# Attention scores in 32-row strips of the array, transposes in one PSUM bank, four rotating banks, and a new written-out order

## The reference

```python
h = tok(x)                                    # (32, 38, 256): layernorm, W, layernorm, + positions
h = h + attn0(layernorm(h))                   # causal; quantised w_attn, w_proj
h = h + tanh(layernorm(h) @ weight @ aux1 @ aux2 + bias)
h = h + attn1(layernorm(h))                   # not causal; biases, head mask
h = h + moe(layernorm(h))                     # softmax gate, top 1 of 16, capacity 76, two matrices

def attn(x):                                  # per image and head
    att = softmax(q @ k.T / 4 (+ causal mask))     # 38 x 38
    return concat_heads(att @ v) @ w_out
```

## Time and profile before

| | |
|---|---|
| times of three runs without a profile | 348.88, 349.08, 351.28 us; median 349.08 |
| span of the profiled execution, first to last instruction | 353.6 us |
| busy: TensorE, VectorE, ScalarE, GpSimd | 94%, 57%, 48%, 47% |
| instructions | 8931, of them 3254 matmul records and as many weight loads |

### The profile page before, as it was taken

One profiled execution on the slowest core, in us unless ns is written; L12 is line 12 of the kernel. 1 busy time (PEld: TensorE's weight loads), 2 busy tenths in 40 slices (PEclk: granted clock), 3 DMA queues, 4 the chain that ended last, 5 costly groups with the idle time before them and its releaser, 6 DMA issues.

```text
span 353.6 us, 8931 instructions
## 1 busy us (share of the span) xinstructions
PE 331.0 (94%) x3254; PEld 240.4 (68%) x3254; DVE 201.4 (57%) x525; ACT 169.6 (48%) x483; POOL 165.1 (47%) x280
## 2 busy tenths in 40 slices
PE   4979999999889999999999988979999999999993
PEld 3867887878768688888888866768455455464361
DVE  4469588455638856586676799770243351361350
ACT  0568824856246575676665555540243342441340
POOL 2166559946467787498776664661002102012012
PEclk9996999999989999999999999868999999999998
DMA  7999007213464157185312214115999998992400
GB/s 225 412 395 406 21 28 256 72 53 108 135 197 164 58 184 246 57 271 168 112 55 87 83 56 163 50 51 167 390 379 408 344 374 346 340 356 101 149 11 12
DMA packets 40155, 66.24 MB, mean 187 GB/s; under 512 B 4831, under 2 KB 30920, under 8 KB 39760
## 3 DMA queue, kind: packets, MB, share of 16 engines
q1 hardware_dynamic: 35832, 56.37, 46.0%
q10 hardware_dynamic: 2632, 7.05, 5.3%
q0 software_dynamic: 1648, 2.24, 1.9%
HBM read 54.17 MB, written 8.48 MB: 177 GB/s over the span
## 4 chain that ended last, share of the span: by engine, by line
PE 73%; SPq 10%; issue 6%; DVE 5%; POOL 2%; DMA 2%; ACT 1%; DVEq 0%; POOLq 0%; ACTq 0%
PE bank L1101 12%; PE bank L1068 12%; SPq L744 10%; PE bank L932 8%; PE bank L956 6%; PE bank L1023 4%; PE bank L967 4%; PE bank L1079 3%; PE bank L1007 3%; PE bank L986 3%; PE bank L996 3%; PE bank L1030 3%; PE bank L1107 2%; PE bank L941 2%; PE bank L890 2%
## 5 line engine op out<-in xcount | busy, mean ns | idle before, releaser
L857 POOL DMA_INDIRECT out<-mid,idx x12 | 11.7, 976 | 97.9 <-DVE mid L1479 97.0
L1101 PE MATMUL bank<-early,mid 128*64 128x256 f32 (+1 forms) x448 | 43.7, 381 | 0.0
L827 POOL TENSOR_TENSOR mid<-mid,tab 128x608 f32<-128x608 f32 x32 | 38.7, 1211 | 4.5 <-PE bank L986 2.2
L1261 ACT ACTIVATE mid<-bank,cols 128x64 f32<-128x64 f32 (+1 forms) x128 | 25.8, 332 | 25.1 <-PE bank L1079 25.1
L1068 PE MATMUL bank<-early,mid 128*64 128x512 f32 (+1 forms) x192 | 36.2, 596 | 0.7 <-ACT mid L1244 0.7
L1101 PEld LDWEIGHTS bank<-early,mid 128*64 128x64 f32 (+1 forms) x448 | 25.3, 123 | 15.8 <-issue 2.9
L1383 DVE TENSOR_REDUCE mx<-bank 102x16 f32<-102x608 f32 x32 | 25.2, 787 | 17.6 <-PE bank L986 17.3
L956 PE MATMUL bank<-xnT,attn 128*128 128x256 f32 (+1 forms) x160 | 35.1, 372 | 0.0
L956 PEld LDWEIGHTS bank<-xnT,attn 128*128 128x128 f32 x160 | 29.0, 190 | 3.9 <-issue 0.6
L812 POOL TENSOR_TENSOR rs<-rs,mhalf 128x1 f32<-128x1 f32 (+2 forms) x50 | 28.8, 576 | 4.2
L932 PE MATMUL bank<-early 128*128 128x256 f32 (+2 forms) x120 | 29.9, 410 | 0.0
(11 more groups left out here) (153 smaller groups left out, 669.1 us busy)
## 6 DMA issues: line engine op xcount, KB each, us to landing
early<-in_w SPq DMA_DIRECT2D x52, 512.0 KB, 7.1
v3a<-vt SPq DMA_DIRECT2D x102, 40.0 KB
early<-vt SPq DMA_DIRECT2D x90, 40.0 KB
expert_in<-k_empty SPq DMA_DIRECT2D x6, 514.0 KB, 4.9
early<-in_xf SPq DMA_DIRECT2D x4, 768.0 KB, 17.0
early<-in_xt ACTq DMA_DIRECT2D x4, 768.0 KB, 23.0
xnT<-in_w SPq DMA_DIRECT2D x4, 512.0 KB
tokens<-in_w SPq DMA_DIRECT2D x4, 512.0 KB
```

What stands on the lines that cost most here:

```text
L827: eng.tensor_tensor(km[:, n % 2], bc(kT[:, :, n * PCOLS:(n + 1) * PCOLS], 2, 4), bc(bc(quarterm[:, :], 2, PCOLS), 1, KC), ALU.mult).then_i ...
L1101: ins = mm(Yp[m % 2][a * width:(a + 1) * width, 0:DIM], hT[:, m % 2, c, a * width:(a + 1) * width], w2s[e % W2_SLOTS][:, c, :], start=c == ...
L1261: ins = eng.activation(hT[:, m % 2, c, a * width:(a + 1) * width], Tp[0][:, c * 128 + a * width:c * 128 + (a + 1) * width], ACT.Relu, bias ...
```

## The change

Scores go in 32-row strips. `score_order` puts two heads into each 32-row strip of features, `km` holds two copies instead of four, and the scores of a pair are 16 matmuls of 2 x 38 = 76 columns (eight before, of 152), which go to four PSUM banks, one per strip, and two halves of the partitions: eight tiles of the array where there were four. The causal mask of layer 0 comes in two parts of 32 query rows: 16 bf16 matmuls of 152 columns (four before, of 304).

PSUM: four banks `low` for the scores, four banks `high` for a rotation of four. The transposes of the probabilities are packed, 76 columns apart, into one bank, with a permuted identity `pack` that puts the pair's 76 real columns first; `pt` and `pv` have no banks of their own any more and take turns in the rotation. VectorE takes the reciprocal in two halves. The planner knows a cost of switching TensorE between full array, score strips and value product, and all wishes have new numbers, so all lists are new.

```diff
-GOAL = {"exp": 89.3, "z": 175.2, "xs": -251.3, "tabs": -0.2, "cs": -328.8, "bs": 60.1, "asum": 171.8, "qs": -234.6, "fB": -330.4,
+GOAL = {"exp": 118.7, "z": 240.6, "xs": -207.7, "tabs": 174.3, "cs": 34.3, "bs": -74.3, "asum": -274.8, "qs": -1652.0, "fB": 155.3,
...
+MODE, SWITCH = {"s": 1, "pv": 2}, 0.09
...
-           "ffn": "dve", "log": "act", "cnt": "dve", "v": "act", "qk": "act"}
+           "ffn": "dve", "log": "act", "cnt": "dve", "v": "act", "qk": "act", "pt": "act", "pv": "dve"}
...
-    f, r, i, d = np.meshgrid(np.arange(KC), np.arange(2), np.arange(4), np.arange(HD), indexing="ij")
-    return w[..., ((8 * r + 4 * f + i) * HD + d).reshape(-1)]
+    f, g, i, d = np.meshgrid(np.arange(KC), np.arange(4), np.arange(2), np.arange(HD), indexing="ij")
+    return w[..., ((4 * g + 2 * f + i) * HD + d).reshape(-1)]
...
-        return max([at] + [end[d] + (0.06 if d[0] == e else HANDOVER[d[0]]) for d in before])
+        at = max([at] + [end[d] + (0.06 if d[0] == e else HANDOVER[d[0]]) for d in before])
+        return at + SWITCH if e == "pe" and MODE.get(kind, 0) != mode[0] else at
...
-        Sp = bank[0][:, :].rearrange("p (f n) -> p f n", f=2)
-        PTp = bank[1][:, :].rearrange("p (j n) -> p j n", j=8)
-        Op = bank[2][:, 512:1024]
...
-        G = [bank[3][:, 0:512], bank[3][:, 512:1024], bank[2][:, 0:512]]
...
+        Sp = low[:, :].rearrange("p (g n) -> p g n", g=4)
...
+        G = [high[:, 512 * b:512 * (b + 1)] for b in range(SLOTS_G)]
...
                     if l == 0:
-                        for r, r0, r1, q, key in corners:
-                            mm(Sp[r0:r1, r, 0:8 * SEQ], identb[BROW * r:BROW * (r + 1), BROW * r:BROW * r + r1 - r0], causb[BROW * r:BROW * (r + 1), :],
-                               start=True, stop=False, skip_group_check=True)
+                        for part in range(2):
+                            for g, strip, r0, r1, q, key in corners:
+                                mm(Sp[r0:r1, g, 0:4 * SEQ], selb[strip, part, 0:r1 - r0], causb[strip, part, :],
+                                   start=part == 0, stop=False, skip_group_check=True)
                     for f in range(KC):
-                        for r, r0, r1, q, key in corners:
-                            half = slice(BROW * r, BROW * (r + 1))
-                            ins = mm(Sp[r0:r1, r, 4 * f * SEQ:4 * (f + 1) * SEQ], qT[half, f, q], km[half, n % 2, f, :, key],
+                        for g, strip, r0, r1, q, key in corners:
+                            ins = mm(Sp[r0:r1, g, 2 * f * SEQ:2 * (f + 1) * SEQ], qT[strip, f, q], km[strip, n % 2, f, :, key],
                                      start=l == 1, stop=True, skip_group_check=True)
...
-                    if m > 1:
-                        pe.wait_ge(pt_ready, m - 1)
-                    else:
-                        pe.wait_ge(tables_used, 2)
+                    ps, full = take(uses[(kind, l, n)])
                     for j in range(6):
-                        ins = tr(PTp[0:KROWS, j, 0:PROWS], P[0:PROWS, n % 2, HSTART[j]:HSTART[j] + 3, :], ident[0:PROWS, 0:PROWS])
+
+                        ins = tr(ps[0:KROWS, j * PCOLS:j * PCOLS + PROWS], P[0:PROWS, n % 2, HSTART[j]:HSTART[j] + 3, :], pack[0:PROWS, :])
...
-                    link(eng.reciprocal(rec[:, n % 2, :], ov[:, :, HD]))
+                    ov = G[b][0:PROWS, 0:HEADS * VW].rearrange("p (h d) -> p h d", h=HEADS)
+                    eng.reciprocal(rec[0:SEQ, n % 2, :], ov[0:SEQ, :, HD])
+                    link(eng.reciprocal(rec[BROW:PROWS, n % 2, :], ov[BROW:PROWS, :, HD]))
```

More of the change, by code:

```diff
@@ L48 @@
 BROW = 64
+QROW = 32
 PROWS = BROW + SEQ
@@ L68 @@
 SLOTS = 4
+SLOTS_G = 4
 EPS = 1e-5
@@ L83, in constants @@
     head[p, p // HD] = 1.0
-    quarter = np.zeros((128, 4), np.float32)
-    quarter[p, p % BROW // HD] = 1.0
+    twin = np.zeros((128, 2), np.float32)
+    twin[p, p % QROW // HD] = 1.0
     block = np.zeros((KROWS, HEADS), np.float32)
@@ L294, in needs @@
         step("pe", "ffn", 0, t, ("act", "lnt", 1, t), ("act", "fW", 0, 0))
-        step("dve", "ffn", 0, t, ("pe", "ffn", 0, t))
+        step("dve", "ffn", 0, t, ("pe", "ffn", 0, t), *([("dve", "ffnr", 0, t - 2)] if t > 1 else [("dve", "tokn", 0, TILES - 2)]))
         step("act", "ffn", 0, t, ("dve", "ffn", 0, t))
@@ L379, in plan @@
     queues = {}
-    norms, stats, uses, xns = [], [], [], []
+    uses, xns, mode = [], [], [0]
     for e, kind, l, n in sorted(after, key=lambda s: s[2:]):
@@ L394, in begins @@
             m = len(uses)
-            before += [uses[u] for u in ((m - 3, m - 2) if kind == "qk" else (m - 3,)) if u >= 0]
+            before += [uses[u] for u in ((m - SLOTS_G, m - SLOTS_G + 1) if kind == "qk" else (m - SLOTS_G,)) if u >= 0]
         if (e, kind) == ("act", "lnx") and len(xns) >= XNB:
@@ L427, in plan @@
             uses += [(EMPTIES[kind], kind, l, n)] * (2 if kind == "qk" else 1)
-    return orders
+    return orders, end
+@functools.cache
+def plan():
+    return schedule()[0]
 def order(engine):
@@ L1006, in _ @@
                         for a in range(2):
-                            ins = mm(Op[BROW * a:BROW * a + SEQ, h0 * VW:h1 * VW], PTs[0:KROWS, n % 2, j, a * SEQ:(a + 1) * SEQ], Vb[0:KROWS, (m - 1) % 3, a, h0:h1, :], start=True, stop=True)
+                            ins = mm(ps[BROW * a:BROW * a + SEQ, h0 * VW:h1 * VW], PTs[0:KROWS, n % 2, j, a * SEQ:(a + 1) * SEQ], Vb[0:KROWS, (m - 1) % 3, a, h0:h1, :], start=True, stop=True)
+                            if j == 5 and a == 0:
+                                ins.then_inc(full, 1)
                     ins.then_inc(o_full, 1)
                 elif kind == "ot":
-                    pe.wait_ge(on_ready, m)
+                    emptied(pe, uses[("pv", l, n)])
                     ps, full = take(uses[(kind, l, n)])
                     for f in range(2):
-                        ins = tr(ps[:, f * 128:f * 128 + PROWS], On[0:PROWS, n % 2, f * 128:f * 128 + 128], ident[0:PROWS, 0:PROWS])
+                        ins = tr(ps[:, f * PCOLS:f * PCOLS + PROWS], On[0:PROWS, n % 2, f * 128:f * 128 + 128], pack[0:PROWS, :])
                     ins.then_inc(full, 1)
@@ L1214, in _ @@
                         act.wait_ge(o_full, m - 2)
-                    eng.copy(PTs[0:KROWS, n % 2].rearrange("p j (a n) -> p (j a) n", a=2), bank[1][0:KROWS, 0:6 * 128].rearrange("p (x n) -> p x n", n=BROW)[:, :, 0:SEQ]).then_inc(pt_ready, 1)
+                    eng.copy(PTs[0:KROWS, n % 2], G[b][0:KROWS, 0:6 * PCOLS].rearrange("p (j n) -> p j n", j=6)).then_inc(g_free[b], 1)
                 elif kind == "ot":
```

98 lines of the change are left out of this document (51 added, 47 removed), and 8 rows, old and new, of the table GOAL.

## The result

The changed kernel takes 357.49 us (median of 4 runs, 354.24 to 358.25) against 349.28 for the kernel before: a ratio of 1.0194, 95% interval 1.0146 to 1.0242. It is slower, outside my range, where I had forecast 345.4 and given "slower" 0.17. Medians hold all runs of a kernel; ratios leave out those that ran slow at a lower clock.

A forecast was written before the change was run, and what follows sets the result against it. Until 205 us TensorE's steps and SyncE's spread issues were taken to bound the kernel side by side, then VectorE. TensorE's 4.7 us saved minus 1.0 behind gave 3.7: span 349.9, scaled to 345.4 us, range 342 to 348.5.

The forecast's parts named there:

- the sum: Ninth value group to layer 1's pair 10: TensorE 4.7 us less, minus 1.0 behind, so the end moves 3.7 earlier.
- From there SyncE is no hindrance: After the ninth spread group, SyncE's remaining issues end at the earliest at 209.2 us, against 213.86 before.
- The last stage: Behind layer 1's pair 10, VectorE sets the pace; 1.7 us of work done earlier pays for seven reciprocals.
- The scale: Whole kernel: forecast span 349.9 us times 349.08/353.6, unprofiled median over profiled span, gives 345.4 us.
- the head: Layer 0's start: first value projection 8.5 us later, at 54.1; ninth group ends waiting at 110.3, TensorE 1.0 us behind.
- the strips: Score steps of both layers: eight tiles at once save 0.23 us a step, 7.4 us of TensorE for 32 pairs.
- The reciprocals' 1.8 us: VectorE: 32 more reciprocals of 0.25 us, hidden until 205 us; some seven pairs behind it cost 1.8 us.
- The changes of tiling: TensorE switching between full array, score strips and value product: 95 times instead of 114, 1.9 us less.
- (a): SyncE does not hold layer 0 back, so 11.8 us of TensorE savings count: 337.4 us; chance 0.20.
- (b): Layer 0: waits at value copies lower the clock; ninth copy after 121 us instead of 113: 353.3 us; chance 0.12.
- (c): VectorE's last stage holds the end; 3.7 us of lead arrive as 0 to 1.5: 347.6 to 349.1; chance 0.13.
- (d): Score steps: matmuls in eight tiles start one after another, 15.7 us more, 362.7 us scaled; chance 0.05.

The follow-up runs named there:

- x1: The changed kernel, unchanged, profiled a second time; 358.80 us.
- r1: The changed kernel with three layer-0 value projections moved forward in the lists of TensorE and ScalarE; 352.67 us median, four runs in two pairs.
- r2: The changed kernel with four buffers of copied value rows instead of two; 356.30 us.
- s1: The changed kernel with value rows spread through a DRAM scratch, four or five SyncE issues a group instead of nine; 342.76 us, ratio 0.9805.
- r3: The changed kernel with spreads through DRAM and scores, masks and masked keys back in 64-row strips; 348.93 us, ratio 0.9953.
- x2: The changed kernel with spreads through DRAM plus six useless SyncE issues behind each group; 416.44 us.
- e2: The changed kernel's code with the lists of the kernel before; 357.31 us, ratio 1.0216.
- s4: The changed kernel's code with the lists of the kernel before and spreads through DRAM; 352.10 us, ratio 1.0055.
- e4: The changed kernel with a third of each group's spreads issued by ScalarE instead of SyncE; 375.81 us.

## Why the prediction was wrong

Starts on TensorE, of each one's profiled execution, split the time at two score steps that every list has, the steps of pair 10 (`s10`; in layer 0 from its masks on). In layer 1, and at the last gate count, the second profile of before and then the changed kernel read:

```profile
189.61 0.74 PE L986 MATMUL bank<-mid 64*64 64x152 f32 x16
...
233.85 0.24 PE L1045 MATMUL bank<-oh,maskb 76*76 76x32 bf16 x1 [0.70 <-DVE oh L1419]
```

```profile
189.98 0.51 PE L1000 MATMUL low_banks<-mid 32*64 32x76 f32 x32
...
239.87 0.25 PE L1060 MATMUL high_banks<-oh,maskb 76*76 76x32 bf16 x1 [0.76 <-DVE oh L1434]
```

| | s10 of layer 0 | s10 of layer 1 | last gate count | s10 to s10 | from there |
|---|---|---|---|---|---|
| before, second profile | 107.14 | 189.61 | 233.85 | 82.5 | 44.2 |
| changed | 108.68 | 189.98 | 239.87 | 81.3 | 49.9 |
| changed, second profile (x1) | 111.35 | 192.54 | 240.51 | 81.2 | 48.0 |
| changed, early start (r1) | 105.70 | 187.89 | 231.98 | 82.2 | 44.1 |
| changed, four buffers (r2) | 109.08 | 191.54 | 238.03 | 82.5 | 46.5 |
| changed, DRAM (s1) | 102.52 | 180.85 | 223.42 | 78.3 | 42.6 |

The changed kernel's last gate count comes 6.0 us later than in the second profile of before, where the sum had it 3.7 earlier. Of these 9.7 us 0.5 lie ahead of s10 of layer 0, 3.5 between the two steps and 5.7 behind them (3.2, 3.4 and 3.7 in the second profile of the changed kernel).

- **The failed step** is "From there SyncE is no hindrance". From v9 to s10 of layer 1 the sum had TensorE gain 4.7 us; between the two s10 steps 1.2 came, and with SyncE relieved (s1) 4.2. I compared SyncE's earliest end, 209.2, with the end that it had had, 213.86, in place of the time at which a faster TensorE would need the rows. And its queue is longer than I made it: 161.1 us from the first issue to the last for my 153.6, of them 148.6 for the spreads (0.774 us each by the whole timeline, where I used 0.753 from one stretch) and 9.4 for other loads. So it ended at 214.05 (216.68 in the second profile), 1.9 us behind the second profile of before: a queue that is full from end to end had no room to come earlier.
- **The last stage** I had put at VectorE and called even. It lost 5.7 us (3.7 in the second profile), the largest part of the miss. The stop inside a score step is 2.7 us of it (1.9), and its cause is open. The rest, 3.0 (1.8), goes with the late spreads: r2, whose spreads end as late (215.52) and which has no stop, has 46.5 us, 2.3 more than before; with the spreads 7.4 us earlier (r1) it is 44.1, with SyncE relieved 42.6. VectorE is not fuller: 26.46 of 35.00 us, after 27.68 of 32.40.
- **The scale.** 349.08/353.6 was no stretching by the profile but the difference between two executions: that one was some 6 us slower than the median. The sum was one of differences, so without that error it would have given the same 345.4 (349.08 - 3.7); what it hid is that the old spreads can start earlier, at 45.21 us in the second profile.
- **Right,** to within what two executions differ by: the head. v0 of layer 0 stands at 51.47 and 54.41 us in the two profiles (54.1 forecast), 7.8 and 10.7 later than in the second profile of before (8.5), the ninth group starts at 109.88 and 112.44 (110.3), and TensorE's savings up to there do not arrive: ScalarE's copies wait for spreads, and s10 of layer 0 comes 1.5 and 4.2 us later than before (1.0 forecast). **Right in layer 1, half in layer 0:** the strips, 0.23 and 0.12 us a step, 16 x 0.35 = 5.6 us in all for my 7.4; 5 to 6 measured (r3 against s1). The reciprocals' 1.8 us is neither confirmed nor denied. The changes of tiling I have not measured by themselves.
- **Rivals.** (a) fell: SyncE held layer 0. (b) comes nearest in its picture (waits near 75, 90 and 111 us, clock 0.81 from 80 to 95), but not by its own point: the copy of v9 came at 111.14, not behind 117, and the loss fell in layer 1. (c) fell too: TensorE's lead was gone at s10 of layer 1, ahead of the stage where (c) has it lost, and that stage grew without a fuller VectorE. (d) fell: eight tiles run side by side. The Trainium skill's 25 ns between starts (TensorE: Matmul & The Clock Gate, section on the 56 ns gap) does not hold across tiles here: 16 mask matmuls of one record each start within 0.15 us (118.95 to 119.10), under 0.01 us apart on average.

The loss is thus for its larger part SyncE's: it issues nearly without pause from the first spread to the last, and the new lists start it 7.8 us later (10.7 in the second profile). Relieving it turns 1.0194 into 0.9805 (s1), and issues without use bring the loss back (x2). The stop of 1.9 to 2.7 us in the last stage is unexplained. Of the three changes the strips gain 5 to 6 us, and the lists bring the late start. The rest of the code costs more than the strips gain where it runs the old lists (e2 and s4); one wait of 2.2 us at the rotation was seen of that, so that the rotation needs lists made for it is likely and not shown. What the Trainium skill says under Perfetto Trace Analysis, What "DMA-bound" means (an issuing engine's track solid with slices is itself a bound), is what the rows show: 158.0 of 161.1 us, with the other loads.

The version with the spreads through DRAM, new code and new lists, is faster than both kernels: 342.76 us, 0.9805 of before.

## What to carry to other kernels

An engine that only issues DMAs has no busy column; add up its timeline, and where it is full from its first issue to its last, a saving elsewhere comes through only in part until that queue is relieved (here 1.2 of 4.7 us). Compare such a queue's end with when the faster kernel would need it, not with when it ended before. And look at whether the profiled execution is a typical one before anything is scaled by it.

## What the runs showed that I had not expected

- An issue of 40 rows takes 0.75 to 0.77 us whether it goes from buffer to buffer or inside DRAM (x2), but an issue that writes 40 rows in three copies takes 0.41 (1.24 for three) and one that reads a whole group back to 120 partitions 0.32. More rows in an issue were not dearer but cheaper.
- Two queues that issue at once hardly slow each other: beside ScalarE's issues at 0.80 us SyncE's take 0.74 to 0.80 in e4, about what they take alone. What the second queue cost is ScalarE's time.
- In both profiles of the changed kernel TensorE stops after the same 23 records of pair 14's step. A 16 KB instruction transfer starts at 212.7 in the one (the last record ahead of the stop starts at 212.43) and at 214.7 in the other (215.21), each the first for over 13 us, and both times SyncE has issued four weight loads just before. That TensorE ran out of instructions fits this, and was not tested.
